# A decoder layer on one core: the first cross-attention batch prepared inside the tail of self-attention

## The chip, the cores and the metric

The kernel runs on one core of a Trainium2 chip. The metric is device time in microseconds, the median of several executions of the same program. One more execution was recorded by the profiler; its rows are quoted below. PE is TensorE (matmuls), DVE is VectorE, ACT is ScalarE, POOL is GpSimd, SP is SyncE, which issues all DMAs here. Each engine works through its own list of instructions in order and waits on semaphores for the others.

## The reference

One layer of a decoder, post-norm, for 16 batches of 224 rows of width 512, all in float32:

```
x = layernorm(x + self_attention(x))          # 16 heads of 32, causal, shared Wq, Wk, Wv; then Wu, bu
x = layernorm(x + cross_attention(x, ctx))    # one head of 512; ctx has 750 rows per batch
x = layernorm(x + ffn(x))                     # gated recurrence over the 16 batches, then an output gate
```

Cross-attention is q = x Wq' + bq, k = ctx Wk' + bk, v = ctx Wv' + bv, softmax(q k') v. The kernel multiplies Wq and Wk into one matrix M beforehand, so that the scores are (x M + a bias) times the raw context. To keep float32's accuracy, most operands are split into a rounded high part and a low remainder, and a product is three products: high x high, low x high, high x low.

## The kernel before, in words

Three blocks run one after the other: self_attention, cross_attention, feed_forward. Between two blocks all engines meet; PE's first instruction of a block comes after the last of the block before.

**Self-attention** goes in steps. A step n is one batch b = n // 4 and one group g = n % 4 of four heads; there are STEPS = 64 of them. Every engine runs its own list of steps, software-pipelined: at step n, PE (`steps`, L346) does the scores of step n, a piece of the output projection `wu` of an earlier batch between all groups, PV of step n-3, the transposes `t` of the probabilities of step n-2 (units 1 and 2) and n-1 (unit 0), and every second step the query product `z` of the next pair of groups. Transposes use two PSUM banks by turns; unit 1 of step n-2 and unit 0 of step n-1 use the same one. `w(first, last)` is the place between two groups; during the first two batches `early(n, first)` (L336) computes prepared weights there: steps 0 and 1 the products for Wu, steps 2 to 6 four matmul pieces each for the key bias and for the four column blocks of M. The piece numbered 0 waits for DVE's split of the product before (`job_out`, L528), since all use the one bank `ps_w`. DVE's list per step: the split of the last product (early steps), the residual of a projection (L496), reciprocals, row maxima, the low part of the attention output (`yl`, L488), copies of transposes (L482), and the statistics and norm of a finished batch (L503 to L517). ACT's list: exponentials (L401), the high part of the attention output (`yh`, L411), one copy of transposes (L418), the copy of z. POOL normalises probabilities (L617) and computes the power for the norm (`power`, L624).

Steps 64 to 71 are the tail: no new scores, only the last PVs, transposes and the projections of batches 14 and 15. A projection of 13 products fills `ps_w`; the next may start when DVE's residual has read it (`r_done`). So the projections (14,1), (15,0) and (15,1) follow each other with a residual between. The norm of batch 15 ends the block.

**The SP queue** of self-attention (L161 to L224) issues at each batch b `columns(b+1)` (the input of z), `residual_rows(b-1)`, `store(b-3)` and `rows(b+1)` (the input of PV), each behind its wait. Behind the loop it issues the raw context `ct_raw` and `cx_raw` of batch 0 (1500 KB each) and the layer's rows `x1_raw` of batch 0 (448 KB) for cross-attention, and then the steps B-2 to B+2.

**Cross-attention** (L645) begins with batch 0 unprepared: ACT rounds the context (`cth`, L875), POOL subtracts (`ctl`, L1064), PE transposes x1 (`x1_turn`, L778), ACT and DVE split that (L868, L939), PE computes `zt` (48 products, L797), ACT and DVE split z (L888, L962), and PE computes the scores `s(0)` (L824). DVE has computed a row bias (L946) meanwhile. From batch 1 on, the transposes of batch b+1 come behind the scores of batch b. SP loads the next x1 rows when batch b's are used up (x1b, transposes, row bias), the next context when its low part is done, the next `cx_raw` likewise. Behind the loads of batch 2 it loads three weights of the feed-forward block into `raw`.

The probabilities p0 and p1 are SBUF tensors of self-attention alone; ct_hi and ct_lo are tensors of cross-attention alone. `raw` are three weight buffers that stand free between step 8 and the feed-forward loads.

Of the kernel before, what the change touches and what calls it, by code (L numbers as in the profile page):

```python
# [13 lines left out]
F32 = mybir.dt.float32  # L14
# [35 lines left out]
def self_attention(nc, io, x1, raw, raw_in, shared):  # L50
    with ExitStack() as ctx:
# [27 lines left out]
        p0 = sb("p0", [R, NG, G, R])  # L79
        p1 = sb("p1", [R, NG, G, T])  # L80
# [80 lines left out]
        def _(sp):  # L161
# [60 lines left out]
            for b in range(B - 2, B + 3):  # L222
                step(b, b % 2)

        @block.tensor
        def _(pe):
# [109 lines left out]
            def early(n, slot):  # L336
# [3 lines left out]
                if 2 <= n <= 6 and slot < KC:  # L340
                    job(KB + n - 2, slot)
# [4 lines left out]
            def steps(i, odd):  # L346
                b = 2 * i + odd
                for g in range(NG):
# [10 lines left out]

                    s(n, 2 * b + g // 2, odd, g)  # L360
# [20 lines left out]
            for b in range(B - 2, B + 2):  # L381
                steps(b // 2, b % 2)

        @block.scalar
        def _(act):
# [51 lines left out]

            def steps(b, odd):
                for g in range(NG):
# [5 lines left out]
                    pt_copy(n - 2, (g - 2) % NG)  # L445
                    if g == 0:
# [9 lines left out]
            for b in range(B - 2, B + 1):  # L456
                steps(b, b % 2)

        @block.vector
        def _(dve):  # L460
# [86 lines left out]

            def steps(i, odd):
# [25 lines left out]
            for b in range(B - 2, B + 2):  # L574
                steps(b // 2, b % 2)
            norm(B - 1)

        @block.gpsimd
        def _(pool):
# [47 lines left out]
            def steps(b):  # L627
                for g in range(NG):
# [4 lines left out]
                    if g == 3:  # L633
                        power(b - 2)

# [9 lines left out]
def cross_attention(nc, io, x1, x2, raw, raw_in, shared):  # L645
# [5 lines left out]
    with ExitStack() as ctx:  # L651
# [17 lines left out]
        ct_hi = sb("ct_hi", [128, KC, TX + 2], F32R)  # L669
        ct_lo = sb("ct_lo", [128, KC, TX + 2], F32R)  # L670
# [29 lines left out]
        x1t_done = sem("x1t_done")  # L700
        x1th_done = sem("x1th_done")
        x1tl_done = sem("x1tl_done")
        cth_done = sem("cth_done")
        ctl_done = sem("ctl_done")
        cxh_done = sem("cxh_done")
        cxl_done = sem("cxl_done")
        zt_done = sem("zt_done")
        zth_done = sem("zth_done")
        ztl_done = sem("ztl_done")
# [30 lines left out]
        def _(sp):  # L740
# [19 lines left out]
            for i, name in enumerate(("wf_t", "wi_t", "wc_t")):  # L760
                load_weight(sp, raw[i], raw_in[i], io[name])
# [7 lines left out]
        def _(pe):  # L769
# [45 lines left out]
            def s(b):  # L815
                wait(pe, ztl_done, b + 1)
                wait(pe, ctl_done, KC * (b + 1))
                wait(pe, ptl_done, b)
                for c in range(TC):
                    i = 0  # L820
                    for z, x in ((zt_hi, ct_hi), (zt_hi, ct_lo), (zt_lo, ct_hi)):
# [19 lines left out]
            def step(b):  # L841
                if within(b - 1, B):
                    p_turn(b - 1)
                if within(b, B):
# [10 lines left out]
            x1_turn(0)  # L855
# [8 lines left out]
        def _(act):  # L864
# [46 lines left out]
            def step(b):  # L911
                if within(b - 1, B):
                    pth(b - 1)
                if within(b, B):
                    if not (isinstance(b, int) and b == 0):
                        cth(b)
                    zth(b)
# [8 lines left out]
            cth(0)  # L926
            x1th(0)
# [742 lines left out]
```

## Time and profile before

| what | us |
|---|---|
| median of 3 executions | 1570.85 |
| lowest, highest | 1570.66, 1572.43 |
| the profiled execution, time | 1572.29 |
| its span in the profile | 1570.6 |
| PE busy | 1492.5 |
| DVE busy | 811.3 |
| ACT busy | 602.6 |
| POOL busy | 539.1 |

All times in the rows count from the start of the span. Self-attention takes the span up to 411.5 us, cross-attention follows up to about 913, then comes feed-forward. "[3.81 <-DMA a_xt<-in_xt]" behind a row means that the engine stood 3.81 us before it and that the landing of that DMA ended the wait. A row's "x8" joins eight instructions; its length runs from the first start to the last end, and ends of matmuls overlap the next start.

### The profile page before, as it was taken

The numbers are of one execution on the slowest core, as the hardware profiler recorded it, in microseconds if no ns is written. First come the engines' busy times: TensorE is split into PE (matmuls) and PEld (weight loads), VectorE is DVE, ScalarE is ACT, GpSimd is POOL, SyncE is SP. The second block draws the span as 40 slices with busy tenths as digits, with TensorE's granted clock in tenths as the row PEclk, the third lists the DMA queues.
The fourth block names the chain that finished last, engine by engine and source line by source line (L and its number), as shares of the span: only waits on it lengthen the run. The fifth ranks groups of instructions, "written<-read, shape, count | busy, mean of one in ns | idle before, by whom it ended". The sixth has DMA issues, their size and how long they took to land. (4 is left out here: it accounts for less than half of the span.)

```text
span 1570.6 us, 32655 instructions
## 1 busy us (share of the span) xinstructions
PE 1492.5 (95%) x12242; PEld 1327.8 (85%) x12242; DVE 811.3 (52%) x1851; ACT 602.6 (38%) x1882; POOL 539.1 (34%) x426
## 2 busy tenths in 40 slices
PE   7999999999699999999999859999999999999897
PEld 3577777766598999999999759999999999999785
DVE  4478888877455656656666453222112222122487
ACT  4477777775234444444444231111111111111232
POOL 2455545544455566566566202000000000000254
PEclk9999999998899999999999979999999999999998
DMA  5122323251227433433433050000000000000453
GB/s 179 37 66 83 94 84 91 86 161 56 75 99 203 152 129 133 155 121 134 158 118 133 24 161 24 21 12 12 12 12 23 12 12 12 12 12 1 147 163 119
DMA packets 71596, 130.90 MB, mean 83 GB/s; under 512 B 7218, under 2 KB 15410, under 8 KB 71540
## 3 DMA queue, kind: packets, MB, share of 16 engines
q1 hardware_dynamic: 71540, 130.17, 26.4%
q8 instruction: 33, 0.54, 0.1%
q14 instruction: 23, 0.19, 0.0%
HBM read 106.30 MB, written 22.02 MB: 82 GB/s over the span
## 5 line engine op out<-in xcount | busy, mean ns | idle before, releaser
L401 ACT ACTIVATE a_p<-a_ps_s,a_nmax 112x224 f32<-112x224 f32 (+1 forms) x512 | 198.3, 416 | 96.6 <-DVE a_nmax L467 96.6
L617 POOL TENSOR_TENSOR a_p<-a_p,a_rinv 112x896 f32<-112x896 f32 (+1 forms) x128 | 164.8, 1308 | 174.9 <-DVE a_rinv L475 169.2
L1555 POOL MEMSET o_mhalf<- 128x1 f32 x1 | 0.1, 98 | 506.7 <-POOLq L1114 506.7
L1271 ACT ACTIVATE f_gate<-f_ps_gate,f_bias 128x224 f32<-128x224 f32 x192 | 75.3, 444 | 194.1 <-PE f_ps_gate L1234 194.1
L1070 POOL TENSOR_TENSOR x_cx_lo<-s_cx_raw,x_cx_hi 125x512 fp32r<-125x512 f32 x96 | 120.6, 1284 | 73.4 <-ACT x_cx_hi L901 73.4
L1064 POOL TENSOR_TENSOR x_ct_lo<-s_ct_raw,x_ct_hi 128x750 fp32r<-128x750 f32 x64 | 118.7, 1883 | 12.4 <-ACT x_ct_hi L875 12.4
L277 PEld LDWEIGHTS a_ps_t<-identity,a_p 112*112 112x112 f32 x768 | 87.2, 135 | 34.5 <-issue 13.5
L482 DVE COPY a_pt<-a_ps_t 112x448 f32<-112x448 f32 x128 | 79.4, 621 | 67.5 <-PE a_ps_t L277 67.4
L401 ACT ACTIVATION_READ_ACCUMULATOR a_p<-a_ps_s,a_nmax 112x1 f32 x512 | 113.8, 222 | 0.0
L1305 DVE TENSOR_TENSOR f_xt_lo<-f_ps_x,f_xt_hi 128x448 fp32r<-128x448 f32 x16 | 10.0, 624 | 194.7 <-ACT f_xt_hi L1262 194.7
L277 PE MATMUL a_ps_t<-identity,a_p 112*112 112x112 f32 x768 | 107.0, 262 | 0.0
L466 DVE TENSOR_REDUCE a_nmax<-a_ps_s 112x1 f32<-112x224 f32 x256 | 97.3, 380 | 13.4 <-PE a_ps_s L264 13.1
L1261 ACT ACTIVATE f_xt_hi<-f_ps_x 128x448 fp32r<-128x448 f32 x16 | 8.7, 543 | 234.2 <-PE f_ps_x L1200 234.2
L1316 DVE SCALAR_TENSOR_TENSOR f_fresh<-f_gate 128x448 f32<-128x448 f32 x32 | 20.0, 626 | 145.2 <-ACT f_gate L1271 145.2
L1057 POOL TENSOR_TENSOR x_x1b<-s_x_raw,s_bv_all 112x1024 f32<-112x1024 f32 x16 | 38.2, 2385 | 88.9 <-DVE x_r L989 88.9
L467 DVE TENSOR_REDUCE a_nmax<-a_ps_s 112x1 f32<-112x112 f32 x256 | 67.8, 265 | 0.0
L309 PE MATMUL a_ps_w<-a_w_hi,a_yt_lo 128*112 128x512 f32 x128 | 65.1, 522 | 0.0
L977 DVE TENSOR_REDUCE x_smax<-x_ps_s 112x1 f32<-112x750 f32 x32 | 30.1, 939 | 58.6 <-PE x_ps_s L824 58.6
L908 ACT ACTIVATE x_p<-x_ps_s,x_shift 112x750 f32<-112x750 f32 x32 | 28.4, 888 | 75.7 <-DVE x_shift L982 75.7
L810 PE MATMUL x_ps_g<-x_pt_hi,x_cx_hi 125*128 125x224 f32 x384 | 53.4, 274 | 3.2 <-DVE x_pt_lo L955 3.2
L946 DVE CUSTOM_DVE_ANT_0 x_dot<-s_x_raw,s_kbias 112x512 f32<-112x512 f32 x32 | 54.6, 1706 | 0.5
L1564 POOL TENSOR_TENSOR o_r<-o_h,o_x_raw 128x512 f32<-128x512 f32 x28 | 36.2, 1292 | 52.7 <-ACT o_h L1495 52.7
(221 smaller groups left out, 4043.9 us busy)
## 6 DMA issues: line engine op xcount, KB each, us to landing
s_ct_raw<-in_ct SPq DMA_DIRECT2D x16, 1500.0 KB, 7.9
s_cx_raw<-in_cx SPq DMA_DIRECT2D x16, 1500.0 KB
a_xt<-in_xt SPq DMA_DIRECT2D x16, 448.0 KB, 3.9
a_xrow<-in_x SPq DMA_DIRECT2D x16, 448.0 KB, 3.6
a_xres<-in_x SPq DMA_DIRECT2D x16, 448.0 KB, 4.6
x_scratch<-a_xn SPq DMA_DIRECT2D x16, 448.0 KB, 3.1
s_x_raw<-x_scratch SPq DMA_DIRECT2D x16, 448.0 KB, 3.7
x_scratch<-x_xn SPq DMA_DIRECT2D x16, 448.0 KB, 6.2
```

The costliest lines, as they stand in the source:

```text
L277: mm = pe.transpose(ps_t[0:R, (g + unit) % 2, h * R:h * R + R], src, identity[0:R, 0:R])
L309: mm = pe.matmul(ps_w[0:R, :], *products[i], start=(i == 0), stop=(i == len(products) - 1))
L401: e = act.activation((p1 if c else p0)[:, g, h, :], src, ACT.Exp, bias=nmax[:, g % 2, c, h:h + 1], accum_out=rsum[:, g % 2, c, h:h + 1])
L466: dve.tensor_reduce(nmax[:, g % 2, 1, h:h + 1], ps_s[0:R, h, 0:T], AX.X, ALU.max, negate=True)
L467: dve.tensor_reduce(nmax[:, g % 2, 0, h:h + 1], ps_s[0:R, h, T:T + R], AX.X, ALU.max, negate=True)\
L482: dve.tensor_copy(transposed(g, unit), unit_bank(g, unit)).then_inc(ptd_done, 1)
L617: pool.tensor_tensor(p[:, g, :, :], p[:, g, :, :], inv, ALU.mult).then_inc(norm_done, 1)
L810: mm = pe.matmul(pair(ps_g, dk), v[:, j, 128 * dk:128 * dk + 128], q[:, j, :], start=(i == 0), stop=(i == 3 * XC - 1))
L946: dve.tensor_tensor_reduce(out=dot[:], in0=x1_raw[:, c, :], in1=kbias[:], scale=1.0, scalar=0.0, op0=ALU.mult, op1=ALU.add, accum_out=rowd ...
L1064: pool.tensor_tensor(ct_lo[:, k, 0:TX], ct_raw[:, k, :], ct_hi[:, k, 0:TX], ALU.subtract).then_inc(ctl_done, 1)
L1070: pool.tensor_tensor(cx_lo[:, j, :], cx_raw[:, j, :], cx_hi[:, j, :], ALU.subtract).then_inc(cxl_done, 1)
L1271: a = act.activation(gate[:, j, m, :], region(3 * half + j, k2), ACT.Tanh, bias=bias[:, j, m:m + 1], scale=0.5 if j < 2 else 1.0)
```

## The change

The first batch of cross-attention is prepared while the last projections of self-attention run. The first users' buffers are placed in memory that is dead by then: ct_hi and ct_lo lie over p0 and p1 (free when the last transposes are done), the first x1 columns and the first z lie in raw[0] and raw[1], and PE uses the banks ps_s. The semaphores of these steps are now shared between both blocks. In cross_attention all of this is left out for batch 0, and `s(0)` reads z from raw. The wf load into raw[0] gets a wait on the first scores.

Two more edits come with it. SP's step(B-2) is issued ahead of the three loads for batch 0 of cross-attention, and then steps B-1 on. And the four pieces of a prepared weight product (steps 2 to 6), so far one each at places 0 to 3 of a step, all stand at place 1, behind PV.

```diff
 # self_attention, SP
+            step(B - 2, B % 2)
             sp.dma_start(shared.ct_raw[:], ...)
             sp.dma_start(shared.cx_raw[:], ...)
             sp.wait_ge(stored, 16 * (B - 5))
             sp.dma_start(shared.x1_raw[:], ...)
-            for b in range(B - 2, B + 3):
+            for b in range(B - 1, B + 3):
                 step(b, b % 2)
 # PE
-                if 2 <= n <= 6 and slot < KC:
-                    job(KB + n - 2, slot)
+                if 2 <= n <= 6 and slot == 1:
+                    for piece in range(KC):
+                        job(KB + n - 2, piece)
+            def first_turn():
+                pe.wait_ge(shared.x1_in, 16)
+                pe.wait_ge(exp_done, G * STEPS)
+                (8 transposes of x1_raw into ps_s banks 0 and 1; x1t_done)
+            def first_zt(ck):
+                if ck == 0:
+                    pe.wait_ge(shared.x1tl_done, 1)
+                (12 matmuls of M and the x1 columns into ps_s bank 2 + ck // 2; zt_done behind ck 3)
+            def late(n):
+                if n == STEPS + 1:
+                    first_turn()
+                if n == STEPS + 3:
+                    first_zt(0)
+                    first_zt(1)
+                if n == STEPS + 5:
+                    first_zt(2)
+                    if isinstance(n, int):
+                        late(n)
                     s(n, 2 * b + g // 2, odd, g)
 ...
             for b in range(B - 2, B + 2):
                 steps(b // 2, b % 2)
+            first_zt(3)
 # ACT
+            def first_columns():
+                x_hi, _ = shared.x1t_first
+                act.wait_ge(shared.x1t_done, 1)
+                (two copies of 128x448 to x_hi; x1th_done)
+                act.wait_ge(shared.ct_in, 16)
+                act.wait_ge(t_done, 3 * STEPS)
+                for k in range(KC):
+                    act.activation(shared.ct_hi[:, k, 0:TX], shared.ct_raw[:, k, :], ACT.Copy).then_inc(shared.cth_done, 1)
                     pt_copy(n - 2, (g - 2) % NG)
+                    if isinstance(n, int) and n == STEPS + 1:
+                        first_columns()
 ...
+            first_z()            # behind all steps: waits zt_done, four activations with zbias; zth_done
 # DVE
+                    if isinstance(n, int) and n == STEPS + 2:
+                        first_columns_low()     # waits x1th_done, two subtractions; x1tl_done
 ...
+            first_z_low()        # behind all steps: waits zth_done, four subtractions; ztl_done
             norm(B - 1)
 # POOL
                     if g == 3:
                         power(b - 2)
+                    if isinstance(n, int) and n == STEPS + 3:
+                        first_context_low()     # four subtractions to ct_lo, each behind its cth_done
 # cross_attention
             for i, name in enumerate(("wf_t", "wi_t", "wc_t")):
+                if i == 0:
+                    sp.wait_ge(s_done, TC)
                 load_weight(sp, raw[i], raw_in[i], io[name])
-            x1_turn(0)           # PE; zt(0) is left out of step(0) too
-            cth(0)               # ACT; zth(0) is left out of step(0) too
-            x1th(0)
-            x1tl(0)              # DVE; ztl(0) is left out of step(0) too
-                    ctl(b)       # POOL, now for b > 0 alone
+                    if not (isinstance(b, int) and b == 0):
+                        ctl(b)
```

## Rows read from the trace of the kernel before

**Rows 1.** The page's slices of 39.3 us, granted TensorE clock in tenths
```profile
PEclk9999999998899999999999979999999999999998
```

**Rows 2.** Timeline of PE, 306 to 369 us: start, length, work, [idle before <-releaser]
```profile
318.31 0.91 PE L237 MATMUL a_ps_z<-a_xt,a_a_diag 128*128 128x448 f32 x2
...
328.96 0.91 PE L237 MATMUL a_ps_z<-a_xt,a_a_diag 128*128 128x448 f32 x2
...
354.39 1.86 PE L237 MATMUL a_ps_z<-a_xt,a_a_diag 128*128 128x448 f32 x2 [3.81 <-DMA a_xt<-in_xt]
...
367.89 0.91 PE L237 MATMUL a_ps_z<-a_xt,a_a_diag 128*128 128x448 f32 x2
```

**Rows 3.** Timeline of SP's issues, 306 to 350 us
```profile
310.88 0.39 SPq L166 DMA_DIRECT2D a_xt<-in_xt  x1
...
328.96 9.95 SPq L221 DMA_DIRECT2D s_x_raw<-x_scratch  x1
338.96 1.26 SPq L166 DMA_DIRECT2D a_xt<-in_xt  x1
...
348.98 0.31 SPq L172 DMA_DIRECT2D a_xrow<-in_x  x1
```

**Rows 4.** Waits from 20 to 84 us: us in total, times, longest us
```profile
PE a_ps_w L331 <- DVE s_m_lo L537: 2.2, 3, 0.8
```

**Rows 5.** Timeline of all engines at the seam, 411 to 429 us
```profile
411.68 2.99 ACT L875 ACTIVATE x_ct_hi<-s_ct_raw 128x750 fp32r<-128x750 f32 x4 [14.36 <-PEq L51]
...
412.02 1.75 PE L778 MATMUL x_ps_g<-identity,s_x_raw 112*128 112x112 f32 x8 [5.38 <-POOL x_ct_lo L1052]
414.23 7.43 POOL L1064 TENSOR_TENSOR x_ct_lo<-s_ct_raw,x_ct_hi 128x750 fp32r<-128x750 f32 x4
...
427.89 1.61 PE L824 MATMUL x_ps_s<-x_ct_hi,x_zt_hi 128*112 128x376 f32 x6 [3.11 <-DVE x_zt_lo L962]
```

**Rows 6.** The tile of x1's rows: its loads, from issue to landing
```profile
DMA to landing us min/median/max: 3.5/3.7/23.5
```

**Rows 7.** Timeline of all engines, 386 to 412 us, the engines beside PE
```profile
386.55 2.81 POOL L617 TENSOR_TENSOR a_p<-a_p,a_rinv 112x896 f32<-112x896 f32 x2
...
388.03 1.61 DVE L517 TENSOR_SCALAR a_xn<-a_r,a_mv,a_rstd 112x512 f32<-112x512 f32 x2
...
396.96 0.36 ACT L411 ACTIVATE a_yt_hi<-a_ps_z 128x224 fp32r<-128x224 f32 x1 [1.28 <-PE a_ps_z L292]
...
406.67 0.69 DVE L496 TENSOR_TENSOR a_r<-a_ps_w,a_xres 112x512 f32<-112x512 f32 x1 [3.44 <-PE a_ps_w L309]
...
409.90 1.00 DVE L517 TENSOR_SCALAR a_xn<-a_r,a_mv,a_rstd 112x512 f32<-112x512 f32 x2 [0.86 <-POOL a_rstd L624]
```

**Rows 8.** Busy time by stretch: us, each engine (x instructions), PEclk, DMA share, GB/s
```profile
44.30:45.01 0.71, 0.71 (x17) 0.42 (x16) 0.71 (x4) 0.41 (x3) 0.71 (x1) 1.00 0.00 0
52.00:60.00 8.00, 7.47 (x47) 3.51 (x46) 4.29 (x13) 3.61 (x18) 4.39 (x4) 0.57 0.00 0
391.00:395.00 4.00, 4.00 (x28) 2.56 (x29) 1.02 (x2) 0.36 (x1) 0.00 (x0) 0.57 0.25 80
```

**Rows 9.** The page's costliest groups: busy, mean ns of one | idle before
```profile
L482 DVE COPY a_pt<-a_ps_t 112x448 f32<-112x448 f32 x128 | 79.4, 621 | 67.5 <-PE a_ps_t L277 67.4
...
L946 DVE CUSTOM_DVE_ANT_0 x_dot<-s_x_raw,s_kbias 112x512 f32<-112x512 f32 x32 | 54.6, 1706 | 0.5
```

**Rows 10.** Timeline of PE in the tail, 386 to 412 us
```profile
390.92 0.58 PE L309 MATMUL a_ps_w<-a_bu_split,a_two_rows_r 128*112 128x512 f32 x1 [1.80 <-DVE a_r L496]
...
399.10 0.46 PE L309 MATMUL a_ps_w<-a_bu_split,a_two_rows_r 128*112 128x512 f32 x1 [0.88 <-DVE a_r L496]
...
403.37 0.46 PE L309 MATMUL a_ps_w<-a_bu_split,a_two_rows_r 128*112 128x512 f32 x1 [1.02 <-DVE a_r L496]
```

**Rows 11.** Timeline of PE, 420 to 426 us, query product
```profile
423.73 0.61 PE L797 MATMUL x_ps_h<-x_x1t_hi,s_m_lo 128*128 128x224 f32 x4
424.18 0.60 PE L797 MATMUL x_ps_h<-x_x1t_lo,s_m_hi 128*128 128x224 f32 x4
```

More of the change, by code:

```diff
@@ L546, in early, with first_columns_low, first_z_low @@
                     job_out(KB + n - 3)
+            def first_columns_low():
+                x_hi, x_lo = shared.x1t_first
+                dve.wait_ge(shared.x1th_done, 1)
+                for k in (0, 2):
+                    v = dve.tensor_tensor(x_lo[:, k:k + 2, :], ps_s[:, k // 2, 0:2 * T].rearrange("p (k t) -> p k t", k=2),
+                                          x_hi[:, k:k + 2, :], ALU.subtract)
+                v.then_inc(shared.x1tl_done, 1)
+            def first_z_low():
+                z_hi, z_lo = shared.zt_first
+                dve.wait_ge(shared.zth_done, 1)
+                for k in range(KC):
+                    v = dve.scalar_tensor_tensor(out=z_lo[:, k, :], in0=ps_s[:, 2 + k // 2, (k % 2) * T:(k % 2) * T + T],
+                                                 scalar=shared.zbias[:, k:k + 1], in1=z_hi[:, k, :], op0=ALU.add, op1=ALU.subtract)
+                v.then_inc(shared.ztl_done, 1)
             def steps(i, odd):
@@ L818, in s @@
                 wait(pe, ptl_done, b)
+                z_hi, z_lo = shared.zt_first if isinstance(b, int) and b == 0 else (zt_hi, zt_lo)
                 for c in range(TC):
                     i = 0
-                    for z, x in ((zt_hi, ct_hi), (zt_hi, ct_lo), (zt_lo, ct_hi)):
+                    for z, x in ((z_hi, ct_hi), (z_hi, ct_lo), (z_lo, ct_hi)):
                         for k in range(KC):
@@ L843, in step @@
                     p_turn(b - 1)
-                if within(b, B):
+                if within(b, B) and not (isinstance(b, int) and b == 0):
                     zt(b)
@@ L1021, in step @@
                     statistics(b - 2)
-                if within(b, B):
+                if within(b, B) and not (isinstance(b, int) and b == 0):
                     ztl(b)
@@ L1598 @@
     stored: object
+    p0: object
+    p1: object
+    ct_hi: object
+    ct_lo: object
+    x1t_first: object
+    zt_first: object
+    x1t_done: object
+    x1th_done: object
+    x1tl_done: object
+    zt_done: object
+    zth_done: object
+    ztl_done: object
+    cth_done: object
+    ctl_done: object
 def decoder(nc, io, out):
@@ L1613, in decoder @@
         identity = sb("identity", [128, 128])
+        raw_at = [nc.sbuf_base + 4 * KC * D * i for i in range(3)]
         raw = [sb(f"w_raw{i}", [128, KC, D]) for i in range(3)]
@@ L1618, in sb2, with at @@
                 return ctx2.enter_context(nc.sbuf_tensor("s_" + name, shape, dt))
+            def at(name, offset, shape, dt=F32R):
+                return nc.alloc_sbuf_tensor_at("s_" + name, shape, dt, offset=offset)
+            CT = 4 * KC * (TX + 2)
+            area_at = nc.sbuf_base
+            area = sb2("area", [128, 2 * CT // 4])
+            p0 = at("p0", area_at, [R, NG, G, R], F32)
+            p1 = at("p1", area_at + 4 * NG * G * R, [R, NG, G, T], F32)
+            ct_hi, ct_lo = (at(f"ct{i}", area_at + i * CT, [128, KC, TX + 2]) for i in range(2))
+            x1t_first, zt_first = (tuple(at(f"first{i}{part}", raw_at[i] + part * 4 * KC * T, [128, KC, T]) for part in range(2))
+                                   for i in range(2))
             shared = Shared(
```

57 lines of the change are left out of this document (43 added, 14 removed).

## The prediction, made before the changed kernel ran

> **What bounds the kernel now.** I read the page's slices first (39.3 us each). TensorE (PE) is busy nearly everywhere, so time can only be won where PE stands or where its clock is low; slices with a PEclk digit of 8 mark such a place, the tenth and eleventh, 353 to 432 us [rows 1]. The digits of 7 and 8 further right lie at stages that the diff leaves alone. Then I read the PE timeline at the places that the diff touches and, beside it, the queue of SyncE (SP) and the other engines.
>
> Three places matter. (1) In batch 14 of self-attention, PE waits 3.81 us for the columns of batch 15 and then works on at half clock: the product that starts at 354.39 takes 1.86 us where it takes 0.91 elsewhere [rows 2]. The SP queue shows why: the columns are issued at 338.96, behind the prefetch of the first cross-attention batch, whose last load held SP for 9.95 us [rows 3]. (2) In steps 4 to 6, PE waits 2.2 us in all, three times, for the split of the product matrix on VectorE (DVE) [rows 4]. (3) At the seam, PE starts cross-attention at 412.02, and the first score product starts only at 427.89, after the chain of transposes, split, query product (PE), split (ScalarE, ACT, then DVE) [rows 5]. The rest of the span is work that the diff doesn't touch.
>
> **Edit 1: the prefetch is issued one step later.** step(B-2) now stands ahead of the three loads. It issues columns(15), residual_rows(13), store(11) and rows(15). In the steady loop the columns of 14 were issued at 310.88, when the scores that free their buffer were done [rows 3]; one batch later, two pairs of 10.65 us [rows 2], is 332.2. Behind the prefetch they landed 15.4 us after their issue; even so they would be there at 347.6, and they are needed at 328.96 + 2 x 10.65 = 350.26. So the wait goes, and with it the low clock that followed. Worth: the pair behind the next starts at 367.89; at the steady pace it would start at 328.96 + 3 x 10.65 = 360.91 [rows 2]. That is 7.0; pairs vary by 0.1, so I take **-6.9 us**. The lower bound is 4.1, the wait alone.
>
> The prefetch itself moves behind rows(15), issued at 348.98 [rows 3], so to 349.3. Its users are in the tail, at 382. The slowest landing of an x1 load was 23.5 us [rows 6]: 350.2 + 23.5 = 373.7, so it is covered. But it now stands ahead of residual_rows(14), store(12) and all after them. SP is free at about 360.2; residual_rows(14) lands by 360.2 + 15.4 = 375.6 and is needed at about 383. Store(12) follows and lands by about 380; DVE's norm(13), which overwrites what it stores, stood at 388.03 [rows 7] and comes to 381.1. That leaves 1 us and is a rival.
>
> **Edit 2: the four pieces of a matrix product stand together behind PV.** The same 20 products are computed. PE reaches the first piece later by the PV group, 0.71 us [rows 8]; three times that covers the waits of 2.2 us in all [rows 4] to about 2.0. Against it: the transpose groups of a step now follow each other with no piece between, and the third writes the bank that the copy of the first (621 ns, [rows 9]) must empty; with one group of 0.3 us between, it waits some 0.35 us in steps 3 and 5 (in 2, 4 and 6 the query product stands between). **-1.3 us**, bounds -2.2 and 0. The low clock from 52 to 60 us [rows 8] comes behind a stretch of one-column products that stays, so I leave it.
>
> **Edit 3: the first batch inside the tail.** I work in the times of before (the shift of 6.9 + 1.3 carries all of it along) and go through the engines in order.
>
> PE: first_turn, 8 transposes, at most 1.75 us as at 412.02 [rows 5] and about half at full clock, falls into the 1.80 us of idle before 390.92 [rows 10] and costs nothing. An idle of 0.9 is left. Idles of 0.88 and 1.02 us in this tail were followed by full-clock products (0.46 us each), the one of 1.80 by a slow one of 0.58 [rows 10] and a clock of 0.57 over 4 us [rows 8], which is 1.7 us of lost work. I take it that step 65 now runs at full clock and ends 1.2 us earlier (some of the 1.7 is filled by waits). If not, that 1.2 comes back.
>
> ACT: behind its last copy of step 65 it now does two column copies (1.0 us) and four context copies (2.99 us, [rows 5]) ahead of yh(63), the last attention output, which is on the path to the last projections. With the copy done at 394.2, yh(63) goes from 396.96 [rows 7] to 398.15 and ends at 398.5. DVE's two subtractions end at 396.4, hidden by this. yl(63) ends at 398.9; residual(14,1), queued behind it, runs to 399.6 (before 398.95).
>
> PE: two z chunks, 24 products at 0.45 us for four [rows 11], take 2.7 us, 397.3 to 400.0. Projection (15,0) starts at 400.0 (before 399.10) and takes 3.25 us (403.37 to 406.67 with the handover, [rows 7, 10]). One more chunk (1.35) ends at 404.6.
>
> DVE: from residual to norm it took 409.90 - 406.67 = 3.23 us [rows 7], so norm(14) starts at 402.1. GpSimd (POOL) now has the four context subtractions (7.43 us, [rows 5]) right behind power(14), so the two run together. For such a meeting the trace has a norm pair of 1.61 us beside a POOL pair of 2.81; alone the norm pair takes 1.00 [rows 7]. I take 1.6: residual(15,0) ends at 404.4, and projection (15,1) starts at 404.6 (before 403.37, [rows 10]), +1.2. The Trainium skill, "SBUF — State Buffer", section "Who interferes with whom", says that a DVE instruction in a 2-port mode and GpSimd exclude each other for a whole instruction. By it the norm could wait out one whole context piece, 7.43/4 = 1.86 us, and this start would be 405.5 rather than 404.6; the row bears out the meeting, but with 0.6 us.
>
> POOL is done with the context at about 409.6, and power(15) is wanted at 410.4, so its queue costs nothing; 0.8 us is the cover. PE: projection (15,1) ends at 407.9, the last chunk at 409.3. ACT's copies and DVE's low parts of z took PE's idle before 427.89, 3.1 us [rows 5]: done at 412.4. They stand ahead of norm(15), which could have started at 411.2; so norm(15) starts at 412.4 (before 409.90), **+2.5 us** on the end of self-attention. Bounds +1.0 (all of it overlaps) and +5 (low clock stays 1.2, the port 0.9, a slow last chunk 0.4).
>
> From norm(15) to PE at the seam stays 2.1 us, and PE goes directly to the scores: 412.02 + 2.5 = 414.5 instead of 427.89. **-13.4 us** net, bounds -14.9 and -10.9. PE comes out of 5.2 us of idle; the scores began at half clock behind 3.1 us of idle too, so I count nothing for that.
>
> Is the gain kept behind it? Row bias on DVE, two products of 1.7 us and one small operation [rows 9], starts at 414 and is done at about 419, before the first scores (420.5). The next x1 load waits for it: issued 419.1, landed 422.8 by the median 3.7 us of [rows 6], wanted when the scores end at 424.4; cover 1.6 us. The next context comes 2 us ahead of its use, its low part is started by then, and the value rows are split by 424.3, wanted at 436. All else in the cross loop keeps its distance from the scores. The added wait on s_done ahead of the wf load is met long before SP comes to it.
>
> **Sum.** -6.9 - 1.3 - 13.4 = -21.6 us. The profiled execution took 1572.29 (span 1570.6 and 1.7 around it), 1.44 above the median of 1570.85. 1572.29 - 21.6 = 1550.7; against the median 1549.3. I give 1549.5.
>
> **Rivals.**
> A, a wait in place of the one removed: store(12) or residual_rows(14) lands late behind 3.4 MB, and norm(13) or residual(14,0) stalls DVE, with copies and the projection behind it. For: the columns took 15.4 us behind that same prefetch. Against: 1 us and 7 us of cover. Price about 3 us: 1552.5. The Trainium skill, "DMA: Bandwidth & Descriptors", section "Queues, rings and completion order", has each ring's descriptors consumed in order; the trace agrees, since the columns landed last of the four [rows 2, 3].
> B, the tail or the restart costs more: low clock stays at 391, the port holds norm(14), and x1 of batch 1 is late for its transposes. Price 1.2 + 0.9 + 1.5 = 3.6: 1553.
> C, edit 2 backfires: the transposes of a step come too late for the copies, 0.7 us (one copy) in each of five steps instead of a gain of 1.3: 1554.5.
> D, the low clock of 52 to 60 us goes as well, since the waits beside it shrink: 8 us at 0.57 [rows 8] are 3.4 us: 1546.
> E, slower: PE stands at first_turn for x1 of batch 0, with the last PV, transposes and projections queued behind it. It decides once that load lands more than 21.6 us later than needed, after about 404, 54 us after its issue against 23.5 at worst so far. It would then give 1573 and more. That the change brings nothing at all would need the same.
>
> **Numbers.** Forecast 0.60 (own range 1547.0 to 1552.0), D 0.12, A 0.11, B 0.10, C 0.04, E 0.03. The range reaches to D and to A, B and C: 1544.5 to 1554.5. 0.2% is 3.1 us, about what a measurement of this kernel tells from no change: faster 0.96, same 0.01, slower 0.03.
>
> **What would show it.** In the new profile: no wait for a_xt around 350 and pairs of 10.65 us all through; the prefetch issued at about 349; no idle ahead of the matrix pieces in steps 4 to 6; first_turn inside the idle at 382; yh(63) behind the context copies; the block's last norm 5.7 us earlier than before (-8.2 + 2.5), the first score product 21.6 us earlier (406.3), and that distance kept at 500 us. Wrong would be: PE waiting for a_r or a_yt longer than 1.5 us in the tail, DVE waiting for a store at 381, or PE waiting for s_x_raw before the second transposes.

## The result: 11.4 us faster, where 21.6 were forecast

| what | before | changed |
|---|---|---|
| median, us | 1570.76 (4 runs) | 1559.33 (4 runs) |
| lowest, highest | 1569.34, 1572.43 | 1557.35, 1560.02 |
| profiled execution, its span | 1572.29, 1570.6 | 1557.35, 1555.6 |

The ratio is 0.9925, with an interval of 0.9908 to 0.9942. The change makes the kernel faster, but the median lies 4.8 us above the top of the range. The page of the changed kernel, engines' busy time and the line that answers to [rows 1]:

```profile
PE 1485.0 (95%) x12242; PEld 1326.7 (85%) x12242; DVE 815.4 (52%) x1851; ACT 602.1 (39%) x1882; POOL 539.8 (35%) x426
...
PEclk9999999999899999999999879999999999999998
```

Of the two digits of 8 at 353 to 432 us one is left, and a new one stands at 856 to 894 us. Which of the gains were kept is read by following one event after another through both timelines. The forecast column holds what the prediction had won by then.

| start of | before | changed | gain | forecast |
|---|---|---|---|---|
| scores of step 7 | 73.18 | 69.41 | 3.8 | 1.3 |
| product behind the one that waited | 367.89 | 357.56 | 10.3 | 8.2 |
| projection (14,1) | 390.92 | 380.57 | 10.35 | 8.2 |
| projection (15,0) | 399.10 | 388.96 | 10.1 | 7.3 |
| projection (15,1) | 403.37 | 396.03 | 7.3 | 7.0 |
| first scores of cross-attention | 427.89 | 407.24 | 20.65 | 21.6 |
| second query product | 442.39 | 425.61 | 16.8 | 21.6 |
| transposes of x1, batch 3 | 497.35 | 479.03 | 18.3 | 21.6 |
| first transposes of feed-forward | 917.70 | 901.02 | 16.7 | 21.6 |
| last transposes of feed-forward | 1406.90 | 1391.96 | 14.9 | 21.6 |

So the gain was nearly whole at the first scores, and was lost at two places behind them, where the prediction had counted nothing. A third loss sits in the tail, hidden in this table by an early gain that was too large. The rows follow in the order of time.

**The columns** (answer to [rows 2, 3]). SP's issues, then PE's products of the last batches:

```profile
345.70 0.46 SPq L218 DMA_DIRECT2D s_ct_raw<-in_ct  x1
346.21 0.41 SPq L219 DMA_DIRECT2D s_cx_raw<-in_cx  x1
346.66 9.71 SPq L221 DMA_DIRECT2D s_x_raw<-x_scratch  x1
...
346.78 0.91 PE L237 MATMUL a_ps_z<-a_xt,a_a_diag 128*128 128x448 f32 x2
357.56 0.92 PE L237 MATMUL a_ps_z<-a_xt,a_a_diag 128*128 128x448 f32 x2
```

The prefetch goes out at 345.7, behind the columns, and no product waits for a_xt. SP is still held 9.7 us; nobody needed it meanwhile.

**The tail** (answer to [rows 7, 10]). PE's projections and transposes, then DVE's norm(14) and POOL's first context piece in a narrow window, the source line of the two norms, and what follows on DVE:

```profile
378.61 0.93 PE L349 MATMUL a_ps_s<-identity,s_x_raw 112*128 112x112 f32 x8
380.57 0.46 PE L309 MATMUL a_ps_w<-a_bu_split,a_two_rows_r 128*112 128x512 f32 x1 [1.03 <-DVE a_r L553]
388.96 0.46 PE L309 MATMUL a_ps_w<-a_bu_split,a_two_rows_r 128*112 128x512 f32 x1
396.03 0.46 PE L309 MATMUL a_ps_w<-a_bu_split,a_two_rows_r 128*112 128x512 f32 x1 [2.49 <-DVE a_r L553]
...
391.30 2.15 DVE L574 TENSOR_SCALAR a_xn<-a_r,a_mv,a_rstd 112x512 f32<-112x512 f32 x1 [0.80 <-POOL a_rstd L700]
391.34 1.82 POOL L717 TENSOR_TENSOR s_ct<-s_ct_raw,s_ct 128x750 fp32r<-128x750 f32 x1
...
L574 DVE TENSOR_SCALAR a_xn<-a_r,a_mv,a_rstd x2: 1730/1940/2150, 391.3 to 393.4; 112x512 f32<-112x512 f32 x2
...
403.69 1.53 DVE L617 SCALAR_TENSOR_TENSOR s_first<-a_ps_s,s_zbias,s_first 128x224 fp32r<-128x224 f32 x4 [0.46 <-ACT s_first L488]
405.13 1.00 DVE L574 TENSOR_SCALAR a_xn<-a_r,a_mv,a_rstd 112x512 f32<-112x512 f32 x2
```

first_turn does sit in the idle before projection (14,1). The norms of batch 14 took 2.15 and 1.73 us where one takes 0.50 alone [rows 7]: the first ended at 393.45, 0.3 us behind POOL's first piece (393.16), and the second at 395.1, 0.2 us behind the second piece. PE stood 2.49 us for the residual queued behind them.

**The seam and the restart** (answer to [rows 5, 6, 9]). All engines from 406 us, in order of time:

```profile
406.96 0.69 DVE L1029 CUSTOM_DVE_ANT_0 x_dot<-s_x_raw,s_kbias 112x512 f32<-112x512 f32 x1 [0.84 <-PEq L51]
407.14 2.76 POOL L1139 TENSOR_TENSOR x_x1b<-s_x_raw,s_bv_all 112x1024 f32<-112x1024 f32 x1
407.24 9.82 PE L910 MATMUL x_ps_s<-s_ct,s_first 128*112 128x376 f32 x48 [5.08 <-POOL s_ct L1134]
407.70 8.99 DVE L1029 CUSTOM_DVE_ANT_0 x_dot<-s_x_raw,s_kbias 112x512 f32<-112x512 f32 x1
409.86 7.96 POOL L1152 TENSOR_TENSOR x_cx_lo<-s_cx_raw,x_cx_hi 125x512 fp32r<-125x512 f32 x6
...
416.73 1.11 DVE L1033 TENSOR_SCALAR x_rowbias<-x_rowdot,s_qk_bias 112x2 f32<-112x2 f32 x1
417.95 0.32 SPq L828 DMA_DIRECT2D s_x_raw<-x_scratch  x1
...
421.60 1.76 PE L863 MATMUL x_ps_g<-identity,s_x_raw 112*128 112x112 f32 x8 [4.53 <-DMA s_x_raw<-x_scratch]
```

PE goes from the end of self-attention straight to the scores, as the diff says. But the second of DVE's two equal products took 8.99 us, the first 0.69. The load of x1 for batch 1 waits for the row bias behind it, so it goes out at 417.95, and PE stands 4.53 us for it and goes on at half clock (8 transposes in 1.76 us, 0.93 elsewhere).

**The clock at the end of cross-attention.** The same place on PE, the kernel before first:

```profile
887.70 0.93 PE L810 MATMUL x_ps_g<-x_pt_hi,x_cx_hi 125*128 125x224 f32 x6 [3.23 <-DVE x_pt_lo L955]
...
889.81 0.83 PE L810 MATMUL x_ps_g<-x_pt_hi,x_cx_hi 125*128 125x224 f32 x6
```

```profile
869.45 0.93 PE L895 MATMUL x_ps_g<-x_pt_hi,x_cx_hi 125*128 125x224 f32 x6 [3.23 <-DVE x_pt_lo L1038]
...
872.00 1.48 PE L895 MATMUL x_ps_g<-x_pt_hi,x_cx_hi 125*128 125x224 f32 x6
```

Both stand 3.23 us and come back at full clock. Then three groups of the changed kernel run at the lower clock (1.32, 1.48 and 1.41 us for 0.83), which costs it 1.6 us, and none of the kernel before. That and a like place in the second batch of feed-forward (8 transposes in 1.76 us, before 0.99, and 1.5 us lost in all) make up nearly all of the 3.3 us that go between batch 3 and the end. The code is the same there.

### The profile page after: what moved, and what is told of

Read it like the earlier page. It is cut to its first block and busy times, and to the rows that moved or that the text cites. A ratio compares the mean times of both kernels' runs of the same rounds, so it can differ in the third digit from the quotient of the medians.

```text
span 1555.6 us, 32657 instructions
## 1 busy us (share of the span) xinstructions
PE 1485.0 (95%) x12242; PEld 1326.7 (85%) x12242; DVE 815.4 (52%) x1851; ACT 602.1 (39%) x1882; POOL 539.8 (35%) x426
## 5 line engine op out<-in xcount | busy, mean ns | idle before, releaser
L437 ACT ACTIVATE s_p<-a_ps_s,a_nmax 112x224 f32<-112x224 f32 (+1 forms) x512 | 198.4, 417 | 93.2 <-DVE a_nmax L524 93.2
L693 POOL TENSOR_TENSOR s_p<-s_p,a_rinv 112x896 f32<-112x896 f32 (+1 forms) x128 | 164.8, 1308 | 165.7 <-DVE a_rinv L532 160.1
L1146 POOL TENSOR_TENSOR s_ct<-s_ct_raw,s_ct 128x750 fp32r<-128x750 f32 x60 | 111.5, 1888 | 9.0 <-ACT s_ct L960 9.0
L437 ACT ACTIVATION_READ_ACCUMULATOR s_p<-a_ps_s,a_nmax 112x1 f32 x512 | 114.0, 223 | 0.0
L277 PEld LDWEIGHTS a_ps_t<-identity,s_p 112*112 112x112 f32 x768 | 85.6, 134 | 30.2 <-POOL s_p L693 9.1
L277 PE MATMUL a_ps_t<-identity,s_p 112*112 112x112 f32 x768 | 105.2, 260 | 0.9 <-DVE a_pt L539 0.9
L910 PE MATMUL x_ps_s<-s_ct,x_zt_hi 128*112 128x376 f32 x480 | 87.0, 333 | 0.0
L910 PEld LDWEIGHTS x_ps_s<-s_ct,x_zt_hi 128*112 128x112 f32 x480 | 81.2, 175 | 0.2
L1029 DVE CUSTOM_DVE_ANT_0 x_dot<-s_x_raw,s_kbias 112x512 f32<-112x512 f32 x32 | 60.9, 1902 | 1.4 <-PEq L51 0.8
```

Source lines behind the costliest of these rows:

```text
L277: mm = pe.transpose(ps_t[0:R, (g + unit) % 2, h * R:h * R + R], src, identity[0:R, 0:R])
L437: e = act.activation((p1 if c else p0)[:, g, h, :], src, ACT.Exp, bias=nmax[:, g % 2, c, h:h + 1], accum_out=rsum[:, g % 2, c, h:h + 1])
L693: pool.tensor_tensor(p[:, g, :, :], p[:, g, :, :], inv, ALU.mult).then_inc(norm_done, 1)
L910: mm = pe.matmul(ps_s[0:R, 2 * c + half, 0:XH + 1], z[:, k, c * R:c * R + R], x[:, k, half * XH:half * XH + XH + 1], start=(i == 0), stop= ...
L1029: dve.tensor_tensor_reduce(out=dot[:], in0=x1_raw[:, c, :], in1=kbias[:], scale=1.0, scalar=0.0, op0=ALU.mult, op1=ALU.add, accum_out=rowd ...
L1146: pool.tensor_tensor(ct_lo[:, k, 0:TX], ct_raw[:, k, :], ct_hi[:, k, 0:TX], ALU.subtract).then_inc(ctl_done, 1)
```

## The experiments

Each ratio is to the kernel before on the same chip. Gains are compared through these ratios, since not every variant has the changed kernel measured beside it. Of the gain of the first runs the profile is read with the distance from projection (14,1) to the first scores, which leaves the early stages out: 36.97 us before, 26.67 in the changed kernel.

**One edit alone.** Three kernels, each the kernel before with one of the three edits (their diffs are parts of the one above), and the changed kernel once more.

> The kernel before with edit 1 alone: SP's step(B-2) ahead of the three prefetch loads. My theory (the stall at 354 and its low clock go, and nothing late takes their place): the wait for a_xt is gone, the pair period stays at 10.65, first row of cross-attention about 6.7 to 6.9 us earlier, time 6.9 us lower (1563.9), within 1 us. Rival (the gain is given back later, at a store or at a low clock elsewhere): under 4 us lower, with a new wait on a stored row or a residual, or a slower stretch behind 412 us.

> The kernel before with edit 2 alone: the four pieces of a product together behind PV. In the changed kernel the stretch from the scores of step 2 to those of step 7 was 2.3 us shorter, and step 2 itself began 1.5 us earlier, at full clock where the kernel before was at half, before any piece had moved. Theory (the edit is worth the covered waits, and the rest is the clock's chance): 1.3 to 2.3 us lower. Rival (the edit changes the clock too): 3.5 us lower, with step 2 early again.

> The changed kernel with edits 1 and 2 undone, so edit 3 alone. Theory (two collisions of DVE with POOL eat the gain: norm(14) beside the context subtractions, row bias beside x1b and the value rows): 4.5 to 6.5 us lower than the kernel before, with the norm pair at about 3.8 us and the second row-bias product far over 2 us again. Rival (the collisions were chance, or came from the moved prefetch): norm pair at 1.6, row bias at 1.5 to 2.2 each, and 11 to 13 us lower.

> The changed kernel once more, nothing edited. Theory: the collisions are fixed by the order of the instructions, so the norm pair of batch 14 takes 3.8 us and the second row-bias product 9 us again; the clock falls behind the idle at 878 and 929 us are chance and may be elsewhere, worth 1 to 3 us between runs. Rival: the collisions are chance, and their lengths differ by over 1 us from those of the first profile. Time 1557 to 1560 in both.

| kernel | median, us | ratio to 1569.51 (23 runs) | gain, us |
|---|---|---|---|
| edit 1 alone | 1564.78 | 0.9968 (0.9954 to 0.9981) | 4.7 |
| edit 2 alone | 1567.16 | 0.9986 (0.9971 to 1.0000) | 2.4 |
| edit 3 alone | 1561.20 | 0.9941 (0.9926 to 0.9956) | 8.3 |
| all three | 1557.15 | 0.9913 (0.9895 to 0.9932) | 12.4 |

The parts add up to 15.4 where the whole gives 12.4. The whole has an error of some 3 us and the sum a larger one, so no interaction is shown. Edit 1 alone has no wait for a_xt, and its profile has the gain at that place (6.7 us between the products around it). Its time gained 4.7, with an interval of some 3 to 7 that holds both the 6.9 expected and the rival's "under 4", so the time doesn't decide and the profile does. Edit 2 alone shortens step 2 to step 7 from 47.67 to 45.36 us, and the changed kernel has the same 45.36. Its gain in time is barely clear of nothing. Its step 2 did begin early (24.52 us against 25.51), as its rival had it. But edit 3 alone, which leaves the pieces where they were, has that too (24.20), and the last repeat of the changed kernel, which has edit 2, doesn't (25.41). So the early start isn't edit 2's. Edit 3 alone gained 8.3, with an interval of some 7 to 12, more than the 4.5 to 6.5 expected, but it has both collisions in full, and 26.66 us from projection (14,1) to the first scores where the changed kernel has 26.67. DVE's norm pair and second product in the timeline of edit 3 alone:

```profile
395.12 3.81 DVE L572 TENSOR_SCALAR a_xn<-a_r,a_mv,a_rstd 112x512 f32<-112x512 f32 x2 [0.80 <-POOL a_rstd L698]
...
411.51 8.99 DVE L1027 CUSTOM_DVE_ANT_0 x_dot<-s_x_raw,s_kbias 112x512 f32<-112x512 f32 x1
```

The repeat has 3.80 and 8.99 too, to the hundredth. So these two are no accident of one execution, and they come with edit 3. The clock behind the idle of 3.23 us was expected to be chance and to fall elsewhere. It did not: the repeat and the run of edit 3 alone both lose the same 1.6 us there. Only the group at which it falls differs (the first takes 0.96 in the repeat, 1.14 with edit 3 alone).

**Take POOL out of DVE's way.** The theory: DVE and POOL exclude each other where both read SBUF, and the long one wins. The rival: the operations are slow for a reason of their own (another data pattern, PE or the DMA beside them). Two waits on POOL tell: its context pieces start behind norm(14), its value pieces behind the row bias. The waits take nothing out of the work.

```diff
 # POOL, self-attention: first_context_low            (context waits)
+                pool.wait_ge(xn_done, TC * (B - 1))
 # POOL, cross-attention: cxl(b)                      (values wait)
+                if isinstance(b, int) and b == 0:
+                    pool.wait_ge(rowbias_done, 1)
```

> The changed kernel, with POOL's four context subtractions behind norm(14) (a wait on xn_done). Theory (each of the two norm instructions waited out a context piece, 3.80 instead of 1.00 us; PE's 2.5 us of idle before projection (15,1) and its half clock came from that): norm pair 1.0 us, idle before projection (15,1) under 0.3 us, projection at full clock, and from projection (14,1) to the first scores 22.8 us instead of 26.7; time 3.9 us lower than the changed kernel. Rival (the later context subtractions hold power(15) and give it back there): the same idle gone, but norm(15) waits for the power, and under 1.5 us lower.

> The changed kernel, with POOL's six value-row subtractions of batch 0 behind the row bias of batch 0 (a wait on rowbias_done). Theory (POOL kept DVE's second row-bias product out for 8.99 us, and the x1 load, the transposes and everything behind came 3.9 us late through it): second product ends right behind x1b, under 3.5 us; next x1 load issued about 3.5 us after the first scores start instead of 10.7; PE goes from the first scores to the second query product in 14.5 us instead of 18.4; time 3.9 us lower than the changed kernel. Rival (the product was slow by itself, or the load is held by something else): second product still 9 us, or the load still 10 us behind, and no gain.

> Both waits together. Theory: the two losses are independent, so 7 to 8 us lower than the changed kernel, about 19 to 20 below the kernel before. Rival (they overlap, or the x1 store of batch 15 or another load becomes the bound): 4 to 5 us lower.

The context waits: 1554.39, ratio 0.9903 (0.9886 to 0.9920). The norm pair is back at 1.00, projection (15,1) follows without idle, and the distance to the first scores is 22.38, so 4.3 us less. In time this is 15.2 us below the kernel before. The changed kernel has 12.4 in its repeat, so the time moved by less than the 3.9 expected, and the two intervals overlap. The distance shows the mechanism, the time alone would not:

```profile
392.59 1.00 DVE L574 TENSOR_SCALAR a_xn<-a_r,a_mv,a_rstd 112x512 f32<-112x512 f32 x2 [0.80 <-POOL a_rstd L700]
...
394.64 0.40 PE L309 MATMUL a_ps_w<-a_bu_split,a_two_rows_r 128*112 128x512 f32 x1
...
404.71 8.98 DVE L1030 CUSTOM_DVE_ANT_0 x_dot<-s_x_raw,s_kbias 112x512 f32<-112x512 f32 x1
```

The values wait: 1559.62, 0.9935 (0.9918 to 0.9952), no gain against the changed kernel (0.9913 in its repeat), where 3.9 us were expected. The mechanism answers, the time doesn't:

```profile
408.84 2.75 DVE L1029 CUSTOM_DVE_ANT_0 x_dot<-s_x_raw,s_kbias 112x512 f32<-112x512 f32 x1
411.63 0.23 DVE L1033 TENSOR_SCALAR x_rowbias<-x_rowdot,s_qk_bias 112x2 f32<-112x2 f32 x1
...
408.39 11.11 PE L910 MATMUL x_ps_s<-s_ct,s_first 128*112 128x376 f32 x48 [5.08 <-POOL s_ct L1134]
419.33 0.93 PE L863 MATMUL x_ps_g<-identity,s_x_raw 112*128 112x112 f32 x8
```

The product now waits for x1b alone and PE no longer waits for x1. From the first scores to the second query product it is 16.7 us instead of 18.4. But the scores took 11.11 us here (9.82 in the changed kernel), since the clock stayed low longer behind the same idle of 5.08, and the query product behind them ran at the low clock too. Up to the transposes of batch 4 nothing of it is left: from the first scores it is 101.9 us here, and 101.1 and 101.9 in the two profiles of the changed kernel so far (98.7 in the kernel before).

Both together: 1553.30, 0.9898 (0.9882 to 0.9914), 16.3 us below the kernel before. Expected were 19 to 20, which lies outside the interval; the second wait added about 1 us to the first, within the error. The distance to the second query product is 17.2, that to batch 4 is 102.8. What is late now is an operation on one column, which waits out the whole of the next x1b:

```profile
413.17 2.24 DVE L1063 TENSOR_TENSOR x_biased_max<-x_smax,x_rowbias 112x1 f32<-112x1 f32 x1
...
413.06 2.34 POOL L1140 TENSOR_TENSOR x_x1b<-s_x_raw,s_bv_all 112x1024 f32<-112x1024 f32 x1
```

Alone that operation takes 0.16.

**The order at the end of the tail.** The prediction put 1.2 us on the low part of z standing ahead of norm(15). In the kernel with both waits, the two are exchanged.

```diff
+            norm(B - 1)
             first_z_low()
-            norm(B - 1)
```

> As the one with both waits, and DVE's norm(15) ahead of its z low parts. My prediction took the z low parts ahead of norm(15) to cost 1.2 us on the seam. Theory now (both must be done before the block ends, and DVE is not free in between): no difference over 0.5 us in the distance from projection (15,1) to the first scores. Rival (what the prediction said): 1.2 us shorter.

1553.36, 0.9898 (0.9882 to 0.9915). From projection (15,1) to the first scores it is 9.51 us against 9.61:

```profile
400.64 1.00 DVE L574 TENSOR_SCALAR a_xn<-a_r,a_mv,a_rstd 112x512 f32<-112x512 f32 x2 [0.81 <-POOL a_rstd L700]
401.56 1.52 DVE L617 SCALAR_TENSOR_TENSOR s_first<-a_ps_s,s_zbias,s_first 128x224 fp32r<-128x224 f32 x4
```

The end of the block waits for whichever comes second, and the order doesn't matter. This doesn't say that the low part of z is free. In the changed kernel the power for norm(15) is done at 404.00, and the norm starts at 405.13, behind the low part:

```profile
403.31 0.69 POOL L700 TENSOR_TENSOR a_rstd<-a_veps,a_mhalf 112x2 f32<-112x2 f32 x1 [5.10 <-DVE a_veps L566]
```

So the low part holds the norm up by 1.1 us, near the 1.2 of the prediction. With the order exchanged the norm goes first, the low part comes behind it, and the end is the same.

**x1b behind the short operations.** In the kernel with both waits, POOL also holds x1b(0) until the row bias is done and x1b(1) until the shifts are.

```diff
 # POOL, cross-attention, ahead of the x1b of batch b
+                    if isinstance(b, int) and b == 0:
+                        pool.wait_ge(rowbias_done, 1)
+                    if isinstance(b, int) and b == 1:
+                        pool.wait_ge(shift_done, TC)
```

> The kernel with both waits, and two more on POOL: x1b of batch 0 behind the row bias of batch 0, x1b of batch 1 behind the row maxima of batch 0. With both waits the distance from the first scores to the second query product was 17.2 us, since two one-column operations of the row maximum stood beside POOL (1.22 and 2.24 us, one of them a whole x1b long). Theory (each of DVE's two-input operations waits for POOL's instruction to end): second product 0.7, one-column operations 0.2, and 14.5 us from scores to product; 2 to 3 us lower than with both waits. Rival (the length is the clock's, since the scores themselves took 10.2 us): 16 us or more.

> The changed kernel once more, beside the version with four waits on the same chip: collisions as before (3.80 and 8.99 us), time 1555 to 1560, and 4 to 7 us above the version with four waits.

1550.82, ratio 0.9881 (0.9863 to 0.9899): 19.4 us below the kernel before (1570.24, 11 runs). The changed kernel beside it measured 1556.61, 0.9918 (0.9902 to 0.9933), so the waits together are worth 5.8 us, clear of the error. Four are written; the one ahead of the value pieces has nothing left to do, since x1b(0), which stands ahead of them, waits for the same row bias. From the first scores to the second query product it is 15.7 us, between the 14.5 of the theory and the 16 of the rival. From the first scores to the transposes of batch 4 it is 98.6, as in the kernel before (98.7): here the loss at the restart is gone, by this and by a clock that stays up at batch 3. The restart in it, DVE and POOL:

```profile
403.01 0.69 DVE L1030 CUSTOM_DVE_ANT_0 x_dot<-s_x_raw,s_kbias 112x512 f32<-112x512 f32 x1 [0.84 <-PEq L51]
403.74 0.69 DVE L1030 CUSTOM_DVE_ANT_0 x_dot<-s_x_raw,s_kbias 112x512 f32<-112x512 f32 x1
404.79 2.37 POOL L1140 TENSOR_TENSOR x_x1b<-s_x_raw,s_bv_all 112x1024 f32<-112x1024 f32 x1 [1.55 <-DVE x_rowbias L1034]
407.12 7.52 POOL L1155 TENSOR_TENSOR x_cx_lo<-s_cx_raw,x_cx_hi 125x512 fp32r<-125x512 f32 x6
410.56 2.86 DVE L1063 TENSOR_TENSOR x_biased_max<-x_smax,x_rowbias 112x1 f32<-112x1 f32 x1
413.46 1.19 DVE L1066 TENSOR_TENSOR x_shift<-x_rowbias,x_biased_max 112x1 f32<-112x1 f32 x1
```

Both products take 0.69. What is left: the one-column operations at 410.56 and 413.46 now meet the value pieces instead (2.86 and 1.19 us for 0.16 each). The wait for x1 at batch 3 stays (1.48 us, 1.50 in the changed kernel). The changed kernel run beside this one has the collisions again (3.79 and 8.96 us).

**Why 8.99 us.** A product that waits out one instruction of POOL would take at most 2.8 us more, the length of x1b. This one was issued beside x1b and got in only behind five of the six value pieces, 6.8 us past the end of x1b. One theory (A): DVE gets in when POOL passes from one instruction to the next, if the moment is right, so another order or more boundaries shorten it. The other (B): an operation that met x1b is held for a time that the pieces don't set. Two variants of the changed kernel tell, one with POOL's value pieces of batch 0 ahead of x1b(0), one with each piece cut in two (12 pieces of 256 columns).

```diff
 # POOL, step(0): order                     # POOL, cxl(0): halves, for each row piece j
+    if isinstance(b, int) and b == 0:      +    tensor_tensor(cx_lo[:, j, 0:256], ...)
+        cxl(b)                             +    tensor_tensor(cx_lo[:, j, 256:512], ...)
+        residual_bias(b, odd)
+        return
```

> The changed kernel with POOL's six value-row subtractions of batch 0 ahead of x1b of batch 0, and no wait added. Is it the value rows that keep the second row-bias product out, or x1b? Theory A (DVE gets in at the next boundary of POOL's, and x1b's length did the rest): both products done within 4 us. Theory B (DVE does not get in between these short pieces): the second product again stands for most of the 7.5 us of pieces, 6 to 10 us.

> The changed kernel with the value rows of batch 0 subtracted in twelve halves of 256 columns. Theory A (it is a matter of boundaries, one more every 0.65 us gives DVE more chances): second product done in under 5 us. Theory B (a boundary between ready pieces lets nothing in): still over 8 us, up to the end of the pieces.

Values first, the second product and POOL beside it:

```profile
407.47 7.98 POOL L1152 TENSOR_TENSOR x_cx_lo<-s_cx_raw,x_cx_hi 125x512 fp32r<-125x512 f32 x6 [0.42 <-ACT x_cx_hi L986]
407.57 1.73 DVE L1029 CUSTOM_DVE_ANT_0 x_dot<-s_x_raw,s_kbias 112x512 f32<-112x512 f32 x1
```

Half pieces, the same:

```profile
404.80 8.95 DVE L1029 CUSTOM_DVE_ANT_0 x_dot<-s_x_raw,s_kbias 112x512 f32<-112x512 f32 x1
...
412.48 0.73 POOL L1153 TENSOR_TENSOR x_cx_lo<-s_cx_raw,x_cx_hi 125x256 fp32r<-125x256 f32 x1
413.17 1.19 POOL L1154 TENSOR_TENSOR x_cx_lo<-s_cx_raw,x_cx_hi 125x256 fp32r<-125x256 f32 x1
414.31 0.74 POOL L1153 TENSOR_TENSOR x_cx_lo<-s_cx_raw,x_cx_hi 125x256 fp32r<-125x256 f32 x1
```

Issued beside a value piece, the product gets in at the first boundary. Issued beside x1b, it ends 6.8 us behind x1b's end (407.0 with halves, some 409.9 in the changed kernel) either way, past five boundaries between pieces or past nine; the half piece that it meets is stretched from 0.73 to 1.19. So more boundaries don't help, which speaks for B. But the pieces have a part in it: with none queued behind x1b the product came out at x1b's end (2.75 us, the values wait). What sets the 6.8 us isn't shown by any run and stays open. Neither variant shows a change of the end: 1555.46 and 1555.39, one execution each, within the range of the changed kernel's own (1553.1 to 1560.2). With the values first, x1b came at 415.41 and the load of x1 waited for that instead; PE stood 4.58 us.

## Why the prediction was wrong, step by step

Two of the signs that the prediction named for being wrong came true: PE waited 2.49 us for a_r in the tail, and 4.53 us for s_x_raw before the second transposes.

**Right.** Edit 1: forecast 6.9, measured 10.33 - 3.65 = 6.7 between the product before the stretch (3.65 gained by 304 us) and that behind it. Rival A fell: no store or residual input was late behind the prefetch. first_turn cost nothing, and projection (14,1) came at full clock. Edit 2: the bank wait came as told (0.35 forecast, 0.42 in the row below), but the sum was mis-sized by 1.0: 2.3 gained, a tenth beyond the bound of 2.2. Another 1.5 us of the early gain is luck, not the change's: at 22.6 us, ahead of every moved piece, a pair of products took 1.13 us in the changed kernel and 2.07 before, behind the same idle. In the two further profiles of the changed kernel the pair took 1.19 and 2.08. Rivals C and E didn't happen.

```profile
38.59 0.57 PE L277 MATMUL a_ps_t<-identity,s_p 112*112 112x112 f32 x4 [0.42 <-DVE a_pt L539]
```

**Failed: norm(14), priced at 1.6.** I took the nearest row, a pair of norms that met the end of a POOL pair [rows 7]. It measured 3.80. The row showed one partial meeting (1.61 where the pair takes 1.00 alone); here POOL's pieces stood back to back and each of the two norms waited out one. With it came 2.5 us of idle and a half-clock projection. The seam gained 20.65 - 10.33 = 10.3 instead of 13.4: 1.8 of the difference lies ahead of projection (15,1), 1.3 behind it. The run with the context waiting gives 36.97 - 22.38 = 14.6, 1.2 more than forecast: so the meeting was the whole shortfall of the seam, and the other terms of it were too high by 1.2 in sum. Of these, 0.7 lie between projections (14,1) and (15,0), which stand 8.38 us apart and not 9.08, and the rest in small parts behind that. The 1.2 us for z's low part held (1.1 measured).

The Trainium skill, "SBUF — State Buffer", section "Who interferes with whom", has this rule, and the prediction weighed it at 0.9 us and put it aside for the row. The measurement decides for the rule: each norm waited for its own piece, 2.8 us more for the pair, which is nearly twice the 1.5 that I worked out from it, since I let only one of the two wait. For the product at the restart the rule falls short: it gives one instruction of POOL, x1b, and the product ended 6.8 us behind that.

**Failed: "Is the gain kept behind it?"** The row bias was to be done about 5 us after its start, from the mean of 1706 ns [rows 9], and the x1 load was to have 1.6 us of cover. The load went out at 417.95 instead of 410.9 (419.1 less the shift of 8.2). The gain fell by 3.9 us there, of which 1.5 came back by batch 3, half of it because the changed kernel waits less for x1 there (1.50 us against 2.29). This is the mechanism of rival B, which had 0.10 and a price of 1.5 for it, and 0.9 for the norm; B's two collisions came true, and its time of 1553 was too low. The sign was there to read. The kernel before has, at its own seam:

```profile
416.63 1.46 DVE L946 CUSTOM_DVE_ANT_0 x_dot<-s_x_raw,s_kbias 112x512 f32<-112x512 f32 x1
418.13 2.15 DVE L946 CUSTOM_DVE_ANT_0 x_dot<-s_x_raw,s_kbias 112x512 f32<-112x512 f32 x1
420.33 1.35 DVE L950 TENSOR_SCALAR x_rowbias<-x_rowdot,s_qk_bias 112x2 f32<-112x2 f32 x1
```

Two columns in 1.35 us is no work, it is a wait (0.23 with POOL idle), and so is most of a mean of 1706 ns for an operation that takes 0.69 alone. I used the mean as a cost that moves along unchanged, but it belongs to the neighbour, and the change put it beside another one, x1b.

**Failed: the clock of untouched stages.** I left it as it was. The profiled execution lost 3.3 us to it after batch 3. The idle of 3.23 us stands in all fourteen profiles of this study. From the first to the twelfth group behind it, the kernel before and edit 2 alone take 7.5 us, and the other twelve profiles 9.1, though their first group takes anything from 0.93 to 1.62. The second batch of feed-forward has its transposes at 1.75 us or more in seven profiles, among them all three of the changed kernel, and at 0.99 in the kernel before. So the 1.6 us come back in every repeat, and it isn't shown that they are chance. They may belong to the shifted times of the changed kernels, or the one profile of the kernel before may be a lucky one; a second profile of it would tell. The medians point the same way. By batch 3 the profile had gained 18.3, or 16.8 without the luck at 22.6 us, and the gains in time were 11.4, 12.4 and 13.6. What sets the clock at these places stays open. The kernel before spread over 1564.3 to 1574.7 us in its runs, and my range had nothing for any of this. Rival D tied a clock gain to the early stage; there was one, of 1.5 us, at another place and by chance.

The sum: 21.6 forecast, less 0.95 at the first scores, less 3.9 at the restart, plus 1.5 by batch 3, less 3.3 of clock, is 14.95, the difference of the two profiled executions (1572.29 - 1557.35 = 14.94). It closes because its terms are read from these two. The medians differ by less, 11.4, because the profiled execution of the kernel before was 1.5 above its median and that of the changed one 2.0 below.

## What to carry to other kernels

Where a step is moved beside work of a neighbour that reads the same memory, price it twice: at its length alone, and behind every instruction of the neighbour that it can meet, one by one for each of its instructions. Tiny operations with long times in the profile of before point to such pairs, and a mean over them isn't a cost. Where the bulk worker has slack and the short operations are on the path, let the bulk worker wait: the waits on POOL gave 5.8 us and took nothing out of the work. But count a wait as worth something only when the time shows it: the values wait alone cured its collision and gained nothing. Removing idle from PE can also remove a stretch of low clock, as edit 1 did, and what is left of idle makes a kernel's time uncertain by more than many edits are worth.

## What was not expected of the hardware

- A DVE product of 112x512 takes 0.69 us alone, 1.73 beside the first of short POOL pieces, 2.75 beside x1b with nothing queued behind that, and 8.95 to 8.99 beside x1b with pieces following, whether these have 512 or 256 columns (the half pieces in one profile).
- Operations on a single column wait like large ones: 0.16 us alone, up to 2.86 beside POOL.
- An idle of 1.80 us before the same projection was followed by 0.58 us in the kernel before [rows 10] and by 0.46 in the run of edit 1 alone, and an idle of 2.18 at 22.6 us by 2.07 or 1.13 for the same two products. The Trainium skill, "TensorE: Matmul & The Clock Gate", Part 1, calls the moment at which the clock changes variable from run to run; these rows agree. It meant here that a difference of 2 or 3 us between the ends of two profiles says nothing of an edit. The distance between two near events says more, where the clock beside it is looked at too.
